# A graph and mixture-of-experts layer: where the two expert outputs of a node are weighted and added

## The reference, cut to what matters

```python
gate_logits = xf @ Wg + bg                       # xf = layernorm(x), 3125 x 256
top_w, top_i = jax.lax.top_k(gate_logits, 2)
top_w = jax.nn.softmax(top_w, axis=-1)
w_dense = jnp.sum(jax.nn.one_hot(top_i, E) * top_w[..., None], axis=1)
for e in range(E):                               # E = 8, W1[e] 256 x 1024, W2[e] 1024 x 256
    h = jax.nn.gelu(xf @ W1[e] + b1[e], approximate=False)
    out = out + w_dense[:, e:e + 1] * (h @ W2[e] + b2[e])
return x + out
```

## Time and profile before

| | us |
|---|---|
| median of 3 runs | 1193.23 (1191.24 to 1194.68) |
| the profiled execution's own time | 1193.23 |
| its span, first to last instruction | 1191.5 |
| PE busy | 1054.6 (89%) |
| DVE busy | 765.9 (64%) |
| POOL busy | 635.5 (53%) |
| ACT busy | 630.8 (53%) |

### The profile page before, as it was taken

How to read it: one execution, slowest core, us unless ns; L and a number is a source line. 1 busy time by engine, 2 the same in 40 slices (tenths; PEclk the granted TensorE clock), 3 DMA queues, 4 the chain that set the end, 5 groups by cost and what they waited for, 6 DMA issues and landing times.

```text
span 1191.5 us, 27118 instructions
## 1 busy us (share of the span) xinstructions
PE 1054.6 (89%) x8001; PEld 995.5 (84%) x8002; DVE 765.9 (64%) x1944; ACT 630.8 (53%) x1948; POOL 635.5 (53%) x700
## 2 busy tenths in 40 slices
PE   1264999999999999999998987599999999999993
PEld 1154999999999999999898885599999999999993
DVE  6686889999999999998986557333333333333330
ACT  3216755555555555555554670456555555666550
POOL 2472677777777777777761210244444444444431
PEclk9987999999999999999999898899999999999997
DMA  6531233333333333333330237742222222222224
GB/s 161 159 89 40 68 107 106 110 108 105 109 109 109 106 109 110 105 109 104 102 90 2 87 107 262 281 140 38 36 35 35 35 35 35 35 36 38 36 32 121
DMA packets 47379, 108.52 MB, mean 91 GB/s; under 512 B 13814, under 2 KB 24871, under 8 KB 45160
## 3 DMA queue, kind: packets, MB, share of 16 engines
q0 software_dynamic: 30720, 69.24, 23.6%
q1 hardware_dynamic: 16308, 37.47, 9.7%
q10 hardware_dynamic: 308, 1.28, 0.3%
HBM read 90.88 MB, written 20.27 MB: 93 GB/s over the span
## 4 chain that ended last, share of the span: by engine, by line
PE 43%; POOL 24%; issue 16%; DVE 6%; DMA 5%; ACT 3%; SPq 1%; POOLq 0%; DVEq 0%; ACTq 0%
POOL xg L545 24%; PE ps L944 17%; PE ps L958 16%; DMA w_sb<-in_L_ffn_W 4%; PE ps L794 3%; PE ps L848 1%; PE ps L844 1%; PE ps L928 1%; DMA xg<-xn_rows,idx_st 1%; PE ps L873 1%; PE ps L688 1%; DVE ln_stats L1297 1%; PE ps L845 1%; ACT xn_sb L1000 1%; DVE dev L1357 1%
## 5 line engine op out<-in xcount | busy, mean ns | idle before, releaser
L545 POOL DMA_INDIRECT xg<-xn_rows,idx_st x416 | 424.0, 1019 | 187.1 <-issue 124.9
L794 PE MATMUL ps<-sel,xg 128*128 128x120 f32 x2496 | 300.9, 277 | 9.7 <-DVE agg L1562 8.4
L794 PEld LDWEIGHTS ps<-sel,xg 128*128 128x128 f32 x2496 | 286.7, 192 | 22.7 <-issue 17.5
L944 PEld LDWEIGHTS ps<-xst,w_st 128*128 128x128 f32 x1792 | 210.2, 193 | 5.6 <-issue 2.8
L944 PE MATMUL ps<-xst,w_st 128*128 128x128 f32 x1792 | 210.7, 276 | 2.3 <-ACT ht_sb L1250 1.7
L1250 ACT ACTIVATE ht_sb<-ps,b_cur 128x128 f32<-128x128 f32 x448 | 127.6, 368 | 152.8 <-PE ps L944 152.8
L958 PE MATMUL ps<-w_sb,ht_sb 128*128 x896 | 202.8, 379 | 0.8 <-DVE y_sb L1813 0.8
L615 POOL DMA_INDIRECT sum_rows<-y_sb,put_st x56 | 103.5, 1848 | 161.7 <-DVE y_sb L1816 148.6
L958 PEld LDWEIGHTS ps<-w_sb,ht_sb 128*128 128x128 f32 x896 | 166.7, 191 | 21.4 <-issue 1.2
L1098 ACT ACTIVATE e<-ps,neg_top 128x65 f32<-128x65 f32 x416 | 125.3, 319 | 56.4 <-DVE neg_top L1457 56.2
L1070 ACT ACTIVATE zt<-ps 128x512 f32<-128x512 f32 x104 | 62.8, 604 | 170.0 <-PE ps L709 170.0
(11 more groups left out here) (266 smaller groups left out, 1352.0 us busy)
## 6 DMA issues: line engine op xcount, KB each, us to landing
w_sb<-in_L_ffn_W SPq DMA_DIRECT2D x16, 1024.0 KB, 6.9
xg<-xn_rows,idx_st POOLq DMA_INDIRECT x416, 2.8
x_sb<-in_x SPq DMA_DIRECT2D x5, 560.0 KB
xn_rows<-xn_sb SPq DMA_DIRECT2D x5, 560.0 KB
xn_t<-xn_rows SPq DMA_DIRECT2D x25, 112.0 KB
expert_in_rows<-xf_sb SPq DMA_DIRECT2D x12, 224.0 KB
sum_rows<-x_sb SPq DMA_DIRECT2D x12, 224.0 KB
out<-sum_rows SPq DMA_DIRECT2D x3, 560.0 KB
```

Of the source, the lines that this page charges most:

```text
L545: pool.indirect_dma_start(xg[:, s, tt, M:M + D], None, xn_dram, bass.IndirectOffsetOnAxis(ap=idx_st[:, s, tt:tt + 1], axis=0)).then_inc(ma ...
L794: mm = pe.matmul(ps3[:, s, col:col + n], xg[:, r, tt, lhs0:lhs0 + 128], sel[:, s, lo:lo + n], start=(tt == 0), stop=(tt == TG - 1))
L944: mm = pe.matmul(h_of(c), w1_st[:, s, kc, c, :], xst[:, s, kc, :], start=(kc == 0), stop=(kc == 1))
```

## The change

The expert outputs are no longer weighted in their tile nor added in DRAM. `tile_hot` carries one value for every pair, its number; `moves[:, 1]` becomes the pair's own row in a new DRAM tensor `expert_out_rows` (6250 rows, and further rows for slots that hold no pair), and POOL writes `y_sb` there by an indirect DMA that does not accumulate. It waits, by the parity of the tile, for the last but one of these. The three small DVE operations that make the softmax weights move behind the slot tables and write `top_w`, by node. SP no longer writes the residual to DRAM. At the end SP and ACT load both output rows of every node into `y_all` (125 x 25 x 2 x 256, in the place of the W1 weights), DVE multiplies and adds them onto `x_sb` in 50 operations, and SP stores `x_sb` to `out`, block by block.

```diff
-                for p0, p1 in ((0, 112), (112, P)):
-                    sp.dma_start(sum_rows[p0:p1, tiles[0]:tiles[-1] + 1, :], x_sb[p0:p1, tiles[0]:tiles[-1] + 1, :]) \
-                        .then_inc(sum_started, 16)
-            for h in (0, 1):
-                sp.dma_start(sum_dram[N:N + 128, h * 128:(h + 1) * 128], ones[:, :]).then_inc(sum_started, 16)
...
-            sp.wait_ge(sum_added, 16 * TILES)
+            for s in (0, 1):
+                sp.wait_ge(ys_written[s], 16 * (TILES // 2))
             for b in range(0, NB, 2):
                 for p0, p1 in ((0, 112), (112, P)):
-                    sp.dma_start(out_rows[p0:p1, b * JB:(b + 1) * JB, :], sum_rows[p0:p1, b * JB:(b + 1) * JB, :]) \
+                    sp.dma_start(y_all[p0:p1, b * JB:(b + 1) * JB, :, :], y_rows[p0:p1, b * JB:(b + 1) * JB, :, :]) \
+                        .then_inc(y_taken[b], 16)
+
+            for b in range(NB):
+                sp.wait_ge(summed, JB * (b + 1))
+                for p0, p1 in ((0, 112), (112, P)):
+                    sp.dma_start(out_rows[p0:p1, b * JB:(b + 1) * JB, :], x_sb[p0:p1, b * JB:(b + 1) * JB, :]) \
                         .then_inc(out_written, 16)
...
-                if past(i) or o >= 1:
-                    pool.wait_ge(sum_added, count(pool, 16 * k))
+                if past(i) or o >= 2:
+                    pool.wait_ge(ys_written[s], free)
...
-                pool.indirect_dma_start(sum_dram, bass.IndirectOffsetOnAxis(ap=put_st[:, s:s + 1], axis=0),
-                                        y_sb[:, s, :], None, compute_op=ALU.add).then_inc(sum_added, 16)
+                pool.indirect_dma_start(ys_dram, bass.IndirectOffsetOnAxis(ap=put_st[:, s:s + 1], axis=0),
+                                        y_sb[:, s, :], None, bounds_check=K2 * N + SLOTS - 1,
+                                        oob_is_err=False).then_inc(ys_written[s], 16)
...
-                    mm = pe.matmul(ps1[:, 1, 0:2 * TILES], row_hot[:, s, c, :],
-                                   tile_hot[:, s, c, :, :].rearrange("p v t -> p (v t)"),
+                    mm = pe.matmul(ps1[:, 1, 0:TILES], row_hot[:, s, c, :], tile_hot[:, s, c, :],
...
-                    pe.wait_ge(y_biased, AT_ONCE * i + o)
+                    pe.wait_ge(y_ready, AT_ONCE * i + o)
...
-                dve.tensor_tensor(tile_hot[:, s, :, :, :], tile_eq[:, s, :, :].unsqueeze(2).to_broadcast([P, COLS, 2, TILES]),
-                                  pairs[:, q:q + COLS, :].unsqueeze(3).to_broadcast([P, COLS, 2, TILES]),
+                dve.tensor_tensor(tile_hot[:, s, :, :], tile_eq[:, s, :, :],
+                                  pairs[:, q:q + COLS].unsqueeze(2).to_broadcast([P, COLS, TILES]),
                                   ALU.mult).then_inc(hots_ready, 1)
...
                 dve.tensor_tensor(y_sb[:, s, :], ps1[:, 1, 0:D], b2_bc[:, bass.ds(e, 1), :].rearrange("p e d -> p (e d)"),
-                                  ALU.add).then_inc(y_biased, 1)
-                dve.wait_ge(y_biased, k + 1)
-                dve.tensor_tensor(y_sb[:, s, :], y_sb[:, s, :], slot_w[:, bass.ds(k, 1)].to_broadcast([128, D]),
-                                  ALU.mult).then_inc(y_ready, 1)
+                                  ALU.add).then_inc(y_ready, 1)
...
+            for b in range(NB):
+                dve.wait_ge(y_taken[b], 32)
+                for c, done in ((0, y_first), (1, summed)):
+                    for j in range(b * JB, (b + 1) * JB):
+                        if c:
+                            dve.wait_ge(y_first, j + 1)
+                        dve.scalar_tensor_tensor(out=x_sb[:, j, :], in0=y_all[:, j, c, :], scalar=top_w[:, j, c:c + 1],
+                                                 in1=x_sb[:, j, :], op0=ALU.mult, op1=ALU.add).then_inc(done, 1)
```

More of the change, by code:

```diff
@@ L134, in gps_layer_kernel @@
         rstd2 = sb(ctx, "rstd2", [P, J])
+        top_w = sb(ctx, "top_w", [P, J, K2])
         top_i = sb(ctx, "top_i", [P, J, K2])
@@ L241, in gps_layer_kernel @@
         graph.close()
+        late = ExitStack()
+        y_all = sb(late, "y_all", [P, J, K2, D])
+        late.close()
         w1_sb = sb(ctx, "w1_sb", [128, NE, 2, HID])
@@ L285, in gps_layer_kernel @@
         row_hot = sb(order, "row_hot", [P, 2, COLS, 128])
-        tile_hot = sb(order, "tile_hot", [P, 2, COLS, 2, TILES])
+        tile_hot = sb(order, "tile_hot", [P, 2, COLS, TILES])
         tile_eq = sb(order, "tile_eq", [P, 2, COLS, TILES])
@@ L342, in gps_layer_kernel @@
             sem, ("xst_ps", "xst_sb", "w1_half0", "w1_half1", "h_ps", "ht_ready", "y_ps", "y_ready", "b1_ready"))
-        y_biased, sum_started, sum_added, out_written = map(sem, ("y_biased", "sum_started", "sum_added", "out_written"))
+        ys_written = [sem("ys_written0"), sem("ys_written1")]
+        y_first, summed, out_written = map(sem, ("y_first", "summed", "out_written"))
+        y_taken = [sem(f"y_taken{b}") for b in range(NB)]
         block = ctx.enter_context(nc.Block())
@@ L1264, in _ @@
                 expert_step(0, k)
-            act.wait_ge(sum_added, 16 * TILES)
+            for s in (0, 1):
+                act.wait_ge(ys_written[s], 16 * (TILES // 2))
             for b in range(1, NB, 2):
                 for p0, p1 in ((0, 112), (112, P)):
-                    act.dma_start(out_rows[p0:p1, b * JB:(b + 1) * JB, :], sum_rows[p0:p1, b * JB:(b + 1) * JB, :]) \
-                        .then_inc(out_written, 16)
+                    act.dma_start(y_all[p0:p1, b * JB:(b + 1) * JB, :, :], y_rows[p0:p1, b * JB:(b + 1) * JB, :, :]) \
+                        .then_inc(y_taken[b], 16)
         @block.vector
@@ L1715, in _ @@
             own(dve.tensor_tensor(ranks[:, :, :], ranks[:, :, :], both[:, :, :], ALU.subtract))
-            dve.wait_ge(gap_exp, 1)
-            own(dve.tensor_scalar(gap[:, 0, :], gap[:, 1, :], 1.0, None, ALU.add))
-            own(dve.reciprocal(pair_val[:, 0, :, 1], gap[:, 0, :]))
-            own(dve.tensor_tensor(pair_val[:, 1, :, 1], gap[:, 1, :], pair_val[:, 0, :, 1], ALU.mult))
             dve.wait_ge(rank0_ps, 1)
@@ L1769, in _ @@
             dve.tensor_scalar(moves[:, 0, :], pair_i[:, :], 1, None, ALU.arith_shift_right).then_inc(moves_ready, 1)
-            own(dve.tensor_scalar(spare[:, :], placed, 0.0, None, ALU.is_equal))
-            own(dve.tensor_tensor(spare[:, :], spare[:, :], spare_row[:, :], ALU.mult))
-            own(dve.tensor_copy(slot_w[:, :], ps1[:, 1, TILES:2 * TILES]))
-            dve.wait_ge(moves_ready, 1)
-            own(dve.tensor_copy(node_f[:, :], moves[:, 0, :]))
-            dve.tensor_tensor(moves[:, 1, :], node_f[:, :], spare[:, :], ALU.add).then_inc(moves_ready, 1)
+            own(dve.scalar_tensor_tensor(out=spare[:, :], in0=placed, scalar=0.0, in1=spare_row[:, :],
+                                         op0=ALU.is_equal, op1=ALU.mult))
+            dve.scalar_tensor_tensor(out=moves[:, 1, :], in0=placed, scalar=-1.0, in1=spare[:, :],
+                                     op0=ALU.add, op1=ALU.add).then_inc(moves_ready, 1)
             own(dve.tensor_tensor(ended[:, :, :], iota_tile[0:1, :].unsqueeze(2).to_broadcast([1, TILES, NE]),
@@ L1781, in _ @@
             dve.tensor_scalar(etile[:, :], etile_f[:, :], float(NE - 1), None, ALU.min).then_inc(etile_ready, 1)
+            dve.wait_ge(gap_exp, 1)
+            own(dve.tensor_scalar(gap[:, 0, :], gap[:, 1, :], 1.0, None, ALU.add))
+            own(dve.reciprocal(top_w[:, :, 0], gap[:, 0, :]))
+            own(dve.tensor_tensor(top_w[:, :, 1], gap[:, 1, :], top_w[:, :, 0], ALU.mult))
             dve.wait_ge(etile_ready, 1)
```

22 lines of the change are left out of this document (10 added, 12 removed).

## The result

The changed kernel takes 1218.42 us (median of 4 runs, 1217.83 to 1222.76) against 1193.31 beside it. Over all 13 of its executions the ratio is 1.0227, 95% interval 1.0210 to 1.0243, which is 27 us. It is slower, by 25 us by the medians and 27 by the ratio, where the prediction had 7.9. The profiled execution took 1221.18 us with a span of 1219.4, 27.9 us above the 1191.5 of before.

A forecast was written before the change was run, and what follows sets the result against it. PE was taken to fill the expert tiles, leaving the head and tail chains to matter. Head -6.8, last scatter -1.5 and tail +16.2 sum to +7.9 on 1193.2: 1201.1 us, range 1196 to 1209.

The forecast's parts named there:

- The tail's loads: Tail: 6.4 MB of y_all read at the weight loads' 412 GB/s in 15.5 us, within a tail of 29.0 us.
- the rival of slow loads: Tail: loads run at 261 GB/s, as those of x did; tail 38.0 in place of 29.0, 1210.1 us; chance 0.12.
- DVE under the loads: Tail: DVE's 50 operations take 0.34 us each, 17.0 in all, and have to keep up with the loads.
- both cases, 28.0 and 31.1: Tail length set by DVE: 28.0 us if block 0 lands alone, 31.1 if blocks 0 and 1 land together.
- The stores: Tail: 3.2 MB stored at some 300 GB/s, 10.7 us, as stores of xn_sb ran.
- the rival of cheap stores: Tail: stores at 404 GB/s, loads at 430, tail 25.6 us; with other gains +3.7 or +2.2 (1195.4); chance 0.10.
- The head: One-hot rounds to PE's first product: gather issued 3.5 us earlier, landing at 753.6, a gain of 6.8 us.
- PE's halved columns add nothing: One-hot rounds: DVE paces them, so PE's narrower product gains nothing; DVE's smaller tile_hot gives 2.8 us.
- The gather against the weights: Head: the first gather waits for a turn behind weights; issued before expert 4's, it gains 6.8 us, not 3.5.
- The packet-by-packet rule: First gather: DMA engines alternate between queues, so expert 3's weights would delay it alike; gain only 3.5 us.
- Scatter, tiles, epilogue: Last scatter, without multiplication or accumulation, gains 1.5 us; expert tiles, where PE is full, and epilogue 0 us.

The follow-up runs named there:

- e1_loads128: Changed kernel with each block of y_all loaded by one DMA over 128 partitions in place of 112 + 13: 1214.36 us, ratio 1.0179.
- e6_no_small_loads: Changed kernel without the five 13-partition loads, DVE on 112 partitions, 13 partitions of the result left out: 1214.66 us, ratio 1.0187.
- e4_one_queue: e1_loads128 with all five loads of y_all issued by SP, in order, in place of SP and ACT: 1211.14 us, ratio 1.0151.
- e5_half_combine: e4_one_queue with 25 of DVE's 50 operations, the second choice left out of the sum: 1208.89 us, ratio 1.0145.
- e2_wide_rounds: Changed kernel with the one-hot product 112 columns wide again, by reading the 56 twice: 1215.75 us, ratio 1.0180.
- e7_hold_weights: Kernel before with SP issuing expert 4's weights only after POOL's first four gathers have landed: 1189.02 us, ratio 0.9981.
- e3_copy_tail: Changed kernel with the tail's loads, sums and stores replaced by a DRAM-to-DRAM copy of 3125 rows: 1193.61 us, ratio 1.0003.
- e9_narrow_before: Kernel before with the one-hot product 56 columns wide in place of 112, DVE's tables unchanged: 1306.19 us on a slow chip, ratio 1.0028.
- e10_awake: e7_hold_weights with six idle products on PE added behind the one-hot rounds: 1302.19 us on a slow chip, ratio 0.9992.
- e11_awake_again: Same program as e10_awake, run again on another chip against the kernel before: 1188.5 us, ratio 0.9958.

## Why the prediction was wrong, step by step

*Direction: right.* Slower, and by the tail; the gain in the head could not pay for it.

*The tail's loads: the step that failed.* "Loads into SBUF in long runs ran at 412 GB/s: 15.5 us" took its rate from weight loads, which fill 128 partitions; those of `y_all` go as 112 and 13. They ran at some 300 and, while the 13-partition pieces ran, at 72 to 174 GB/s. The tail was 40.4 us and not 29.0. Of the 11.4, 7.8 are the spread over partitions (`e1_loads128`; 6.0 of it the 13-partition loads, `e6_no_small_loads`), 3.1 are the two queues, by which blocks 0 and 1 land together (`e4_one_queue`), and 0.5 is left. Even the rival of slow loads, with 38.0, was too low, and it named the wrong cause: not small packets among them or freshly written rows, for the same rows load at 430 GB/s over 128 partitions. The other load in the earlier trace rows, of `x` at 261 GB/s, is split as 112 and 13 in the kernel too: the sign was there, and it was put down to the small packets.

Why 112 partitions are slow the runs don't say. The Trainium skill, "SBUF — State Buffer", section "Door 1: The DMA port swizzle (why `[64,N]` ≈ `[32,N]`)", says that the rate goes with how many of 16 ports the partitions reach, and its table puts partitions 112 to 124 on four of them, for which it gives some 109 GB/s. The two dips, 119 and 130 GB/s in the mean of their three us, agree with that, and so do the 430 to 440 with all 128. Partitions 0 to 111 reach all 16 by the table, four of them with half the rows. If the others set the pace, the estimate from that page is 7/8 of the full rate, 376 of 430; the trace has 307, so more is at work than that. Nor does this shape slow every transfer: stores from the same 112 and 13 partitions ran at 409 GB/s in `e5_half_combine`.

*DVE under the loads: mis-sized.* The prediction gave 0.34 us an operation from 25 `BATCH_NORM_STATS2`; an operation with two full inputs takes 0.40, 19.9 us and not 17.0. That made DVE the end of the tail, with blocks 0 and 1 landing as a pair. The prediction had both cases, 28.0 and 31.1, and chose the sum over DMA between them; with 0.40 they are 31 and 34.

*The stores: mis-sized, without effect.* They hid behind DVE, and the last block's took 4.1 us from DVE's end. Where they stand alone and queue up they run at 409 GB/s (`e5_half_combine`), so the rival of cheap stores had the better rate; with the loads as slow as they were it decided nothing.

*The head: the second step that failed.* "PE's halved columns add nothing" left out the clock. The rounds did run at 1.46 us as worked out, but only until the granted clock fell to 0.50; then PE paced them at 2.14. In place of -6.8 the head cost +1.15, 0.65 to the transposes and 0.5 more in the slow first product. With the clock kept, the same head gives -5.3 (`e2_wide_rounds`): 3.0 at the gather for 3.5, its landing 3.8 us after issue for 3.55, and a first product that is slower still (6.53 us). So the sizing was near and the assumption about the clock was not.

*The gather against the weights: right in kind.* It waits for a turn: `e7_hold_weights` and `e2_wide_rounds` both land it in 3.0 to 3.8 us, by keeping it ahead of expert 4's weights. The packet-by-packet rule of the Trainium skill ("DMA: Bandwidth & Descriptors", section "Queues, rings and completion order"), which the prediction set beside it, would by its working have had only 3.5 us to gain; `e2_wide_rounds` had 6.0 at the transposes.

*Scatter, tiles, epilogue: right.* -1.80 for -1.5, -0.35 for 0, and `e3_copy_tail` at 1.0003 leaves no cost elsewhere: the rounds' loss and the scatter's gain cancel there. (The residual writes that left SP's queue were 26, and not 24.)

In sum: 7.9 predicted, + 11.4 in the tail, + 8.0 in the head, + 1.3 ahead of the first weights, most of it in code that is the same, - 0.3 at the scatter and - 0.35 in the tiles give the 27.9 of the profiled pair. Over all executions the difference is 27.1.

## What to carry to other kernels

A rate of DMA read from a trace holds for its shape: before a sum is made from it, compare the partitions, and look for a short piece at the end of a split, which may cost more than its bytes. Sum loads, engine and stores as three lines that each may end last, and ask when the first piece lands, since two queues deliver two halves at the time of the second. And an engine that "adds nothing" because it is not the bound can become it by doing less, when its clock falls with its work, as here.

## What the runs showed of the hardware

- TensorE's clock fell from 1.00 to 0.50 (2.4 to 1.2 GHz) in the middle of a steady row of products, when these became 56 columns wide in place of 112 at a cadence of ten in 1.46 us (changed kernel) or in 1.74 us (`e9_narrow_before`). With 112 columns it stayed at 1.00 at both cadences.
- Loads into SBUF with the engines full: mostly 430 to 440 GB/s over 128 partitions (`e1_loads128`), some 300 over 112 (`e6_no_small_loads`), 72 to 174 while 13-partition pieces run (changed kernel). Stores from SBUF over the same 112 and 13 partitions: 409 GB/s when queued (`e5_half_combine`).
- An indirect gather of 128 rows, issued just ahead of 2 MB of weights or in the midst of them, was there 6.8 and 6.0 us later (kernel before, changed kernel); with the next weights held back it was 3.0 (`e7_hold_weights`).
- One chip ran the kernel before 9% slower (1303.1 us), with granted clocks of 0.91 to 0.92 where the kernel before has 1.00 between 200 and 600 us, and the issue of a gather there at 1.08 us for 1.00 in the mean. From the first weights on, it was as fast as the others: 463.7 us in `e10_awake`, 462.5 in `e11_awake_again`.
